# An expert gate in steps of seven tiles with a list of tokens, and expert rows gathered by GpSimd

## What is computed

```python
gate_logits = x @ gate_w + gate_b
topk_vals, topk_idx = jax.lax.top_k(gate_logits, K)          # K = 2 of E = 16
topk_w = jax.nn.softmax(topk_vals, axis=-1)
h = jax.nn.relu(jnp.einsum('bsh,ehf->bsef', x, w1) + b1)     # 256 -> 512
expert_out = jnp.einsum('bsef,efh->bseh', h, w2) + b2        # 512 -> 256
sel = jnp.take_along_axis(expert_out, topk_idx[:, :, :, None], axis=2)
moe = jnp.sum(topk_w[..., None] * sel, axis=2)
...
xn = _layernorm(x, axis=-1)
```

## Time and profile before

| | us |
|---|---|
| median of 3 runs | 2828.68 |
| the profiled execution | 2825.55 |
| its span, from the first instruction to the last | 2823.5 |
| PE busy | 2306.0 (82%) |
| POOL busy | 1620.7 (57%) |
| DVE busy | 1478.0 (52%) |
| ACT busy | 896.3 (32%) |
| gate, from its first instruction to the next stage's | 1212.3 to 1383.3 |
| experts, from there to the next stage's first gather | 1383.3 to 1816.0 |

### The profile page before, as it was taken

How to read it: one execution, slowest core, us unless ns; L and a number is a source line. 1 busy time by engine, 2 the same in 40 slices (tenths; PEclk the granted TensorE clock), 3 DMA queues, 4 the chain that set the end, 5 groups by cost and what they waited for, 6 DMA issues and landing times. The chain is left out here.

```text
span 2823.5 us, 50917 instructions
## 1 busy us (share of the span) xinstructions
PE 2306.0 (82%) x12841; PEld 1929.9 (68%) x12842; DVE 1478.0 (52%) x4377; ACT 896.3 (32%) x2710; POOL 1620.7 (57%) x2170
## 2 busy tenths in 40 slices
PE   7877777788888666555499999799979999994798
PEld 7655665566666554455488888677758999993798
DVE  8645544445455544478422222277757777776311
ACT  2431222222222111134233333266653433341233
POOL 4837777777777777757564000187856555550233
PEclk9989889888888766855699999899999999996899
DMA  4043333333333333312333333222231111111122
GB/s 153 15 123 103 101 101 102 100 101 101 103 102 102 102 101 103 100 53 87 126 101 115 108 124 114 86 72 73 74 93 37 44 42 45 43 45 52 27 36 31
DMA packets 149395, 235.70 MB, mean 83 GB/s; under 512 B 28475, under 2 KB 110096, under 8 KB 149330
## 3 DMA queue, kind: packets, MB, share of 16 engines
q0 software_dynamic: 55856, 141.65, 17.9%
q1 hardware_dynamic: 77218, 73.40, 8.1%
q10 hardware_dynamic: 16256, 19.93, 2.1%
HBM read 175.04 MB, written 59.82 MB: 83 GB/s over the span
## 5 line engine op out<-in xcount | busy, mean ns | idle before, releaser
L868 POOL DMA_INDIRECT all_XN<-h_table,l_srcI x784 | 775.4, 989 | 244.2 <-issue 237.5
L1068 PE MATMUL gcn_acc<-all_XN,gcn_hot 128*128 128x256 f32 x800 | 264.1, 487 | 130.5 <-DMA all_XN<-h_table,l_srcI 113.7
L1068 PE MATMUL gcn_acc<-all_XN 128*128 128x256 f32 x768 | 250.4, 483 | 117.0 <-DMA all_XN<-h_table,l_srcI 101.3
L1068 PEld LDWEIGHTS gcn_acc<-all_XN,gcn_hot 128*128 128x128 f32 x800 | 182.5, 239 | 192.7 <-issue 100.6
L1068 PEld LDWEIGHTS gcn_acc<-all_XN 128*128 128x128 f32 x768 | 173.1, 236 | 174.3 <-issue 91.2
L1741 POOL DMA_INDIRECT comb_ys<-slots_out,all_slot x98 | 100.2, 1022 | 311.2 <-POOLq L1488 287.9
L1560 ACT ACTIVATE moe_hidden<-moe_hid_ps,moe_b 128x128 f32<-128x128 f32 x420 | 130.7, 364 | 301.2 <-PE moe_hid_ps L1635 301.2
L1635 PEld LDWEIGHTS moe_hid_ps<-moe_xst,moe_w 128*128 128x128 f32 x1680 | 204.4, 193 | 28.2 <-issue 22.1
L1635 PE MATMUL moe_hid_ps<-moe_xst,moe_w 128*128 128x128 f32 x1680 | 207.8, 277 | 17.2 <-issue 16.1
L969 DVE COPY_PREDICATED gcn_last_seen<-gcn_seen_sb,gcn_seen 128x392 f32<-128x392 int32 x98 | 57.6, 587 | 288.2 <-ACT gcn_seen_sb L802 288.2
L802 ACT COPY gcn_seen_sb<-gcn_seen 128x392 f32<-128x392 f32 x98 | 47.6, 486 | 505.4 <-PE gcn_seen L1075 505.4
(11 more groups left out here) (386 smaller groups left out, 4916.3 us busy)
## 6 DMA issues: line engine op xcount, KB each, us to landing
moe_w<-in_e_w ACTq DMA_DIRECT2D x32, 512.0 KB, 4.4
moe_xs<-slots_in SPq DMA_DIRECT2D x106, 128.0 KB
slots_out<-moe_y SPq DMA_DIRECT2D x105, 128.0 KB
all_XN<-h_table,l_srcI POOLq DMA_INDIRECT x784, 2.7
all_X<-in_x SPq DMA_DIRECT2D x7, 896.0 KB, 11.2
z_table<-comb_zb SPq DMA_DIRECT2D x49, 128.0 KB
x_table<-all_XN SPq DMA_DIRECT2D x49, 128.0 KB, 1.7
out<-all_X SPq DMA_DIRECT2D x49, 128.0 KB, 1.7
```

Of the source, the lines that this page charges most:

```text
L868: nc.gpsimd.indirect_dma_start(msg[b][:, c, :], None, self.h_table, bass.IndirectOffsetOnAxis(self.srcI[:, GE * g + c:GE * g + c + 1], 0)) ...
L1068: last = nc.tensor.matmul(acc[b % NA][:, :], hot[b % NH][:, c, :], msg[b][:, c, :], start=(c == 0), stop=(c == GE - 1))
```

## The change

**Gate.** The work on DVE is done for seven tiles at once (CT = 7 tiles in C = 7 chunks): one operation on [128, 7, 16] where there were seven on [128, 16]. The layer norm's statistics stay per tile, ACT applies it straight into XN, and PE still turns and multiplies tile by tile. A chunk is ranked by eight bf16 matmuls. Nothing is scattered: SP writes the normalized rows to `rows_table` in node order (7 DMAs of 896 KB). What the experts read is a list: for tile n and lane p, the number of the token that lies there. It is summed on PE by 98 bf16 matmuls of 256 columns, whose operands mark each token's lane (`low`, `tables`) and tile (`high`). DVE, ACT and POOL make these from the ranks. The zero fills and `tile_row` are gone. The first two experts' weights are asked for during the gate.

**Experts.** POOL gathers each tile's rows from `rows_table` by the list, an indirect DMA of 128 rows of 1 KB, into a ring of two buffers. It waits for the gather before it to land. DVE copies a gathered tile from the ring to `xs` (`take`). `look_up` and `keep` stand between two gathers, once in two tiles. SP asks for the next expert's weights, and ACT does only relus.

The core of the diff:

```diff
+                    for c in range(C):
+                        if c >= 2:
+                            rank(c - 2)
+                        turn(CT * c)
+                        for t in range(CT * c + 1, CT * c + CT):
+                            turn(t)
+                            gate(t - 1)
+                        gate(CT * c + CT - 1)
+                    rank(C - 2)
+                    rank(C - 1)
...
+                    for c in range(C):
+                        pe.wait_ge(high_ready, c + 1)
...
+                        for i in range(PC):
+                            last = nc.tensor.matmul(list_ps[0:MAX_TILES, :, :], high[c % 2][:, :, i], tables[:, c, :, :, i],
...
+                    for c in range(C):
+                        root(c)
+                        if c >= 3:
+                            by_lane(c - 3)
+                        apply(CT * c)
...
-                            nc.gpsimd.indirect_dma_start(self.slots_in, bass.IndirectOffsetOnAxis(row_place[b][:, c:c + 1], 0),
...
+                    def gather(i, p):
+                        after_alone(pool, self.passed, ring_in, 16 * i)
+                        after_alone(pool, self.passed, xs_ready, i - 1)
+                        nc.gpsimd.tensor_copy(row_1[p][:, :], self.listed[:, ds(i, 1)]).then_inc(row_1_ready, 1)
+                        after_alone(pool, self.passed, row_1_ready, i + 1)
+                        nc.gpsimd.indirect_dma_start(ring[:, p * D:p * D + D], None, self.rows_table,
+                                                     bass.IndirectOffsetOnAxis(row_1[p][:, :], 0)).then_inc(ring_in, 16)
...
+                    gather(0, 0)
+                    gather(1, 1)
+                    pool.wait_ge(key_chain, 7)
+                    look_up(0)
+                    with pool.Fori(1, T) as h:
+                        gather(2 * h, 0)
+                        keep(h - 1)
+                        look_up(h)
+                        gather(2 * h + 1, 1)
+                    keep(T - 1)
+                    with pool.Fori(T, npairs) as h:
+                        gather(2 * h, 0)
+                        gather(2 * h + 1, 1)
+                    after_alone(pool, self.passed, ring_in, npairs * 32)
...
-                            after_alone(act, self.passed, y_done, a + 1)
-                            after_alone(act, self.passed, y_ready, a + 1)
-                            weights(e + 1, 1 - p)
...
+                            after_alone(sp, self.passed, y_ready, a + 1)
+                            self.weights(sp, e + 1, 1 - p)
...
+                    def take(i):
+                        after(dve, ring_in, 16 * i + 16)
+                        after(dve, turned_ready, i)
+                        nc.vector.tensor_copy(xs[:, :], ring[:, ds((i % 2) * D, D)]).then_inc(xs_ready, 1)
...
                             turn(i + 1)
+                            take(i + 2)
                             after(dve, y_done, i + 2)
```

More of the change, by code:

```diff
@@ L1225, in gate_stage @@
[L1225 to L1234 removed]
+            pairs = s.sb("pairs", [1, 1])
@@ new lines, in _ @@
+                    dve.wait_ge(ready, 8)
+                    for c in range(1, C + 2):
+                        f, g = c - 2, c - 3
+                        sums(c, 0)
+                        bias(f)
+                        own(g)
+                        moments(c, 0)
+                        sums(c, 1)
+                        best(f, 0)
+                        rank(g)
+                        moments(c, 1)
+                        sums(c, 2)
+                        equal(f, 0)
+                        to_whole(g)
+                        moments(c, 2)
+                        weigh(f, 0)
+                        sums(c, 3)
+                        to_lane(g)
+                        to_window(g)
+                        first(f, 0)
+                        moments(c, 3)
+                        choose(f, 0)
+                        lane_number(g)
+                        sums(c, 4)
+                        leave_out(f)
+                        window_number(g)
+                        moments(c, 4)
+                        best(f, 1)
+                        mark_lane(g)
+                        equal(f, 1)
+                        sums(c, 5)
+                        weigh(f, 1)
+                        moments(c, 5)
+                        first(f, 1)
+                        sums(c, 6)
+                        choose(f, 1)
+                        moments(c, 6)
+                        take(f)
+                        scales(c)
+                        carry(f)
@@ new lines, in gate, with rank @@
+                        last.then_inc(logit_done, 1)
+                    def rank(c):
+                        pe.wait_ge(chosen, CH * c + 13)
+                        after(pe, placed, PL * (c - 2) + 1)
+                        ranks = rank_ps[c % 2]
+                        nc.tensor.matmul(ranks[:, :, :], before[:, :], taken[:, c, 0:CT, :], start=True, stop=False)
+                        for later in range(1, CT):
+                            nc.tensor.matmul(ranks[:, later:CT, :], ones[:, :], taken[:, c, 0:CT - later, :], start=False, stop=False)
+                        nc.tensor.matmul(ranks[:, :, :], ones[:, :], taken[:, c, CT:CT + 1, :].broadcast_to([P, CT, E]), start=False, stop=True).then_inc(ranked, 1)
```

575 lines of the change are left out of this document (318 added, 257 removed).

## The result

| | before | after |
|---|---|---|
| median of 4 runs each, taken together, us | 2829.46 | 2862.93 |
| the profiled execution, us | 2825.55 | 2863.62 |
| its span, us | 2823.5 | 2861.9 |
| gate, to the next stage's first instruction | 171.0 | 143.9 |
| experts, to the combine stage's first DMA | 432.0 | 495.9 |

The changed kernel takes 1.0121 times as long (95% interval 1.0104 to 1.0139): 33.5 us slower. A second run of it beside the kernel before gave 1.0119 (1.0102 to 1.0136). The spans differ by 38.4 us. The gate gives 27.1 us back, the experts cost 63.9, and the other 1.6 us lie in the rest; combine lasts 266 to 267 us in both.

The account below looks back on a forecast made before the run. PE bound the experts' stage, no engine was full in the gate; after the change POOL's gathers would bound the experts. Gate -38 and experts +49 gave +11 us on the median 2828.68: 2840 us, range 2800 to 2880.

Parts of the forecast that it names:

- the steps of the gathers: Experts' stage, sign of being right: POOL's gathers come 4.8 and 4.0 us apart in turns.
- the waits of PE and of DVE's copy: Experts' stage, sign of being right: PE idles before its turn for DVE's copy, which waits for the ring's DMA.
- the gate's clock: Gate, sign of being right: PE's clock there is 0.50, with the gate under 140 us.
- The pair: Experts' loop: POOL needs 8.82 us for two tiles' gathers, against PE's 7.50, and becomes the bound.
- The rival of the short pair: Experts' loop: at low bounds a pair takes 8.5 us, giving -16 us, 2813 us; chance 0.22.
- The stage's sum: Experts' stage: 473.4 us from gathers plus 8 us for weights' bursts, 481.4 us, +49 us (+26 to +90).
- The bursts: Experts' stage: 14 weight transfers delay gathers by 0.6 us each in the mean, 8 us (0 to 31).
- The nine lone gathers at the end: End of the experts' stage: nine more gathers at 3.98 us each, ending at 468.6 us.
- The clock: Experts' stage, rival: PE's granted clock falls in gaps for gathers, some 32 us more, 2872 us; chance 0.17.
- The gate: -38 forecast: Gate: 133 us, -38 (115 to 155 us), with five later chunks of 13.0 us each.
- The list: End of the gate: 98 matmuls at 0.11 us full clock, 0.21 half; 16 us with waits (11 to 35).
- SP's request: Experts' stage: SP asks for weights between stores; ACT no longer holds relus (about 0.7 us per expert start), lost in POOL's bound.

Follow-up runs that it names:

- The run with two in flight: Changed kernel with a ring of four tiles in place of two, POOL waiting only for the gather before last: 2790.98 us, ratio 0.9883.

## Why the prediction was right or wrong

Slower was right, and 2862.93 us lies in the range, but the forecast was 2840: a third of the loss. The experts were mis-sized by 15 us of cost and the gate by 11. Part of it is luck. Up to the list the gate was forecast 16 us too long, and the list 30 us too short. With the first put right and the second left as it was, the same sum gives 2824 us, no loss at all. Of the signs named, the steps of the gathers, the waits of PE and of DVE's copy, and the gate's clock came as said; the gate is not under 140 us, and one sign of being wrong came true, list matmuls over 0.3 us.

**The pair: right.** The forecast was 4.84 and 3.98 us, 8.82 for the pair. The medians of 48 turns are 4.77 and 4.15, 8.92. The landing behind a lone gather is, by 4.15 less 0.98 and 0.2, nearer to 3.0 than to the 2.8 of the earlier trace rows. The rival of the short pair needed 2.7. The estimate of 2.3 us by the Trainium skill's formula ("DMA: Bandwidth & Descriptors", section "Anatomy of one DMA") is not what these rows show. Nor does the hold of a look-up's issue by `take` show, which was priced at up to 20 us: the issue takes 973 to 982 ns in all 49 look-ups, also where `take` runs in it (1686.02 and 1686.20). The run with two in flight shows that this serial chain was the whole loss of the experts' stage: without it the stage is 5.9 us below that of before.

**The stage's sum: +49 forecast, +63.9 measured.** Four terms are each a little short. Gather 2 to gather 98 takes 427.5 us without what the bursts add, where 423.3 was forecast: 4.2 us. The bursts: 0.6 x 14 = 8 forecast, 12.4 by adding what the steps have over the medians, 4.4 more. But 2.7 of the 12.4 are no burst's: in one step, of 8.03 us, POOL stands 3.52 us between the copy of the index and the issue, where it stands 0.79 in the others, and the profile shows nothing that it waits for:

```profile
1700.06 0.98 POOL L1659 DMA_INDIRECT moe_ring<-rows_table,moe_row  x1 [3.52 <-issue]
```

It is there again when the kernel is run again; its cause stays open. The nine lone gathers at the end: 3.98 each forecast, 39.6 us in all measured, 4 us more; the last two steps, behind gathers that serve no tile, are 5.07 and 4.91. From the last issue to the next stage's first fetch (1844.17 to 1852.57): 4.8 forecast, 8.4 measured, 3.6 more. The first gathers were 0.7 us early. Together they are the 15 us. The stage waits for the last gathers, though they serve no tile; why they land later than the others no run tests.

**The clock: it hardly fell.** It is 0.98 over the stage with PE busy 436 of 496 us. Behind the step of 8.03 us, where PE had stood 2.7 us ahead of its turn, it fell to 0.50 for 3.4 us, and nowhere else between the first tile and the last. PE waits 38.6 us in 41 turns of the stage for DVE's copy, 0.9 each; the 20 us of the earlier trace rows, from which the rival was carried over, hold a wait of 2.4 us.

**The gate: -38 forecast, -27.1 measured, out of two errors of opposite sign.** Up to the list I had 111.0 us, and it took 95.0. A tile on PE takes 1.17 us, not 1.5: the turn's 0.69 and the gate's 0.88 of the earlier trace rows overlap by 0.4. So the first two chunks take 18.3 us and not 21.0, and the later ones come every 10.9 to 11.1 us instead of 13.0, 11 us less over five. These are no longer paced by PE but by DVE, which works through its round of 11 us nearly without idle time, 3 us of it held by POOL's product; freed of that, the chunks come every 10.2. The rest of the 16 us is in the first turn and the last ranks, over 1 us each. The chain behind the last ranks was right (8.7 us, 9.2 forecast). The collision of DVE and POOL was not in the sum; it cost 6.4. The list then took 30 us more than forecast, and its turn, the change of stage and the allowance for waits 3 us less.

**The list is the step that failed.** "With 256 columns I take 0.11 at full clock and 0.21 at half" left out how the columns lie; 0.466 was measured, 45.7 us in place of 16 and beyond the upper bound of 35. With both operands dense the same matmuls take just these 0.21 and 0.11 us. Two parts were wrong. The nearest row was of 49 columns and did not show what a stride costs at 256: at the half clock, 0.25 of the 0.466 us. And I let the clock rise after 5 us, by the first tile of the experts. With strided columns it did not in 45 us, with dense ones it did.

**SP's request: a term I gave no price.** I wrote that ACT no longer holding the relus is lost in POOL's bound, and the runs bear that out. What I did not price is where the request falls beside the gathers: asked for by ACT, it costs 19 to 21 us more of the experts' stage, all of it in the landings, and the kernel stands 57 us above the kernel before. Where POOL is the bound, it counts when the burst falls upon a gather, not only how long it is.

## What to carry to other kernels

Two buffers do not make two transfers in flight if the issuer waits for the last landing before the next issue; ask how many are under way and count the landing into every step. A matmul's price by its count of columns held here for dense columns alone, and was less than half of it for columns that lie apart: lay the moving operand dense first, then the weights, and look at what the writer of the dense layout now costs. A request of 1 MB belongs where no small transfer that someone waits for is issued right behind it, be it by the same engine, whose list then holds it up, or by another, where it lands later.

## What the runs showed of the hardware

- A bf16 matmul of 256 moving columns that lie 28 bytes apart takes 0.466 us at the clock of 0.50, whether its weights are dense or not. With dense moving columns it takes 0.22 us at 0.50 and 0.20 at 1.00 with strided weights, and 0.21 and 0.11 with dense ones.
- PE counted as busy for 45.7 us on end, and the granted clock stayed at 0.50. With the dense layouts the clock was 0.50 in the first 14 of the same 98 matmuls and 1.00 from there on.
- DVE's product of 128x112 f32 took 3.30 us beside a POOL product of 128x1792 bf16 and 0.26 to 0.28 alone. POOL took 3.35 us for that product, DVE 1.08.
- DVE's bf16 comparison of 1792 elements took 1.08 us with the repeated operand's repeats outermost and 2.02 us with them innermost.
- A gather of 128 rows issued 1.1 us behind a request for 1 MB was waited for 2.4 us longer than an undisturbed one (4.60 and 2.23 us), and one issued 2.6 us behind such a request 0.9 us longer (3.10 us, the gather at 1504.54).
- The granted clock fell from 1.00 to 0.50 for 3.4 us behind waits of PE of 2.3 and 2.7 us, and from the first tile on stayed at 1.00 in the experts' stage of the kernel before.
